# Attention and quantised feed-forward on one core: zero products in TensorE's idle times, quantisation moved into the setup, bias as a weight row, and later rows of maxima issued by SyncE

## What is computed

```python
x: [1, 2048, 128];  xn = layernorm(x)
# attention: 16 heads of dimension 8, causal the other way round (key >= query)
q, k, v = split(xn @ w_attn + b_attn)
scores = q @ k.T / sqrt(8) + mask        # mask = -log(1 + key - query), -inf where key < query
att = softmax(scores) @ v @ w_proj + b_proj
# feed-forward, all operands quantised to FP4 in blocks of 16 along the last dimension
quant(t): scale = max(max|block| / 6, 1e-12); grid value nearest |t| / scale, times sign and scale
gate = quant(xn) @ quant(w_gate).T       # w_gate, w_up: [352, 128]
up = quant(xn) @ quant(w_up).T
ffn = quant(silu(gate) * up) @ quant(w_down).T     # w_down: [128, 352]
out = x + att + ffn
```

## Time and profile before

| | us |
|---|---|
| median of 3 runs | 683.89 (682.28 to 686.52) |
| profiled execution | 685.19, of it 683.4 in the span of the trace |
| busy: PE, DVE, POOL, ACT | 587.4, 581.5, 509.0, 402.3 |
| mean granted clock of TensorE | 0.953 of 2.4 GHz |

### The profile page before, as it was taken

How to read it: one execution, slowest core, us unless ns; L and a number is a source line. 1 busy time by engine, 2 the same in 40 slices (tenths; PEclk the granted TensorE clock), 3 DMA queues, 4 the chain that set the end, 5 groups by cost and what they waited for, 6 DMA issues and landing times.

```text
span 683.4 us, 11295 instructions
## 1 busy us (share of the span) xinstructions
PE 587.4 (86%) x3788; PEld 264.4 (39%) x3839; DVE 581.5 (85%) x1206; ACT 402.3 (59%) x857; POOL 509.0 (74%) x386
## 2 busy tenths in 40 slices
PE   6998588668989798989898898989898898987895
PEld 6676354233434342433332342343234343342323
DVE  4786497999899999889999999999997999896462
ACT  3657146254565556566575666658564666667692
POOL 6034337885878887776879898789896798898893
PEclk9999799797999999999999999999998999999997
DMA  4344312201000000110000000000000000000000
GB/s 135 88 135 120 109 31 57 60 4 68 1 2 3 1 0 3 39 47 2 1 1 1 3 17 0 2 2 1 2 1 1 17 1 1 2 2 1 1 2 16
DMA packets 14717, 16.69 MB, mean 24 GB/s; under 512 B 1594, under 2 KB 14171, under 8 KB 14243
## 3 DMA queue, kind: packets, MB, share of 16 engines
q1 hardware_dynamic: 13859, 15.56, 8.2%
q10 hardware_dynamic: 800, 0.40, 0.2%
HBM read 11.75 MB, written 4.01 MB: 23 GB/s over the span
## 4 chain that ended last, share of the span: by engine, by line
PE 43%; POOL 23%; DVE 13%; ACT 8%; issue 7%; DMA 3%; ACTq 2%; SPq 1%; POOLq 0%; DVEq 0%
POOL ring L763 16%; PE psum L1357 10%; PE psum L1315 9%; PE psum L1339 7%; DVE mxp L1098 5%; DMA qop<-parts_dram 3%; ACT ring L915 3%; PE psum L1290 2%; PE psum L1207 2%; POOL xw L781 2%; POOL xw L779 2%; DVE ring L1125 2%; ACTq L927 2%; PE psum L1275 2%; POOL xw L783 2%
## 5 line engine op out<-in xcount | busy, mean ns | idle before, releaser
L763 POOL TENSOR_TENSOR ring<-ring,dist 128x1024 f32<-128x1024 f32 (+3 forms) x209 | 410.6, 1985 | 109.5 <-ACT ring L915 108.7
L1098 DVE TENSOR_REDUCE mxp<-psum 128x1 f32<-128x512 f32 (+3 forms) x640 | 356.3, 599 | 38.3 <-PE psum L1318 18.8
L915 ACT ACTIVATE ring<-psum 128x512 f32<-128x512 f32 (+3 forms) x418 | 199.7, 527 | 133.6 <-PE psum L1342 74.4
L1315 PE MATMUL psum<-kop,qop 96*128 96x512 bf16 (+3 forms) x640 | 205.3, 361 | 19.6 <-DMA qop<-parts_dram 7.4
L1339 PE MATMUL psum<-qop,kop 128*128 128x512 bf16 (+3 forms) x590 | 182.4, 354 | 20.6 <-ACT ring L915 7.9
L1357 PE MATMUL psum<-ring,vaug 128*32 128x512 f32 (+3 forms) x1280 | 154.1, 552 | 17.9 <-POOL ring L763 16.1
L915 ACT ACTIVATE psum<-psum 128x512 f32<-128x512 f32 (+3 forms) x222 | 113.2, 546 | 59.1 <-PE psum L1339 27.6
L1125 DVE TENSOR_TENSOR ring<-psum,dist 128x512 f32<-128x512 f32 (+3 forms) x222 | 133.5, 625 | 15.2 <-ACT psum L915 14.3
L1315 PEld LDWEIGHTS psum<-kop,qop 96*128 96x128 bf16 x640 | 58.3, 99 | 139.5 <-DVE mxp L1098 48.7
L1339 PEld LDWEIGHTS psum<-qop,kop 128*128 128x128 bf16 x640 | 59.9, 99 | 103.9 <-DVE ring L1125 24.0
L1318 PE MATMUL psum<-tri_q,identb 128*128 128x128 bf16 x256 | 57.3, 225 | 0.0
(11 more groups left out here) (132 smaller groups left out, 508.9 us busy)
## 6 DMA issues: line engine op xcount, KB each, us to landing
kop<-parts_dram SPq DMA_DIRECT2D x9, 384.0 KB
qop<-parts_dram SPq DMA_DIRECT2D x9, 384.0 KB
parts_dram<-qpart SPq DMA_DIRECT2D x18, 128.0 KB, 2.9
xin<-_attn_hidden_states_dram SPq DMA_DIRECT2D x4, 256.0 KB, 4.6
ring<-inv_dram SPq DMA_DIRECT2D x1, 1024.0 KB, 5.0
out_dram<-xin SPq DMA_DIRECT2D x4, 256.0 KB, 2.3
qop<-mrow ACTq DMA_DIRECT2D x48, 4.0 KB
parts_dram<-qpart SPq DMA_DIRECT2D x6, 96.0 KB
```

Of the source, the lines that this page charges most:

```text
L763: g_.tensor_tensor(slot(p)[:, :, 0:n], slot(p)[:, :, 0:n], both, ALU.mult).then_inc(weighed_pool, 1)
L915: a_.activation(scores if pair_vec[p] else slot(p)[:, e % 2, 0:n], scores, ACT.Exp, scale=SCALE).then_inc(exp_done, 1)
L1098: v_.tensor_reduce(mxp[:, u % 2, 4 * a + j, c - g:c - g + 1], bank(*o)[:, 0:n], AX_X, ALU.max).then_inc(max_used, 1)
L1315: ins = mm(bank(*o)[:, 0:n], qop[0:K_MAX, u // NQ % 2, h, P * a:P * (a + 1)], kop[0:K_MAX, h, k0:k0 + n], start=True, stop=(c != g))
```

## The change

1. PE may take products of zeros (`keep`, at most 4,000): a 128 by 128 bf16 tile of zeros with the identity, added to `OUT_BANK`. They have the last rank, and the plan takes one only where by its clock PE has had nothing for 200 ns and a unit's sum is open, that is between the first and the last `pv` of a unit. They wait for nothing.
2. Quantisation: no due time, rank 6.5 (a maximum has 4 when DVE is behind its schedule, 7 when it is ahead, a weighing 5); x pieces wait for their own transpose, the weights for their load; the order is x, x, weights, weights, x, x; the constant goes to the buffer of `hT` instead of `qc`, one buffer for all pieces; POOL's three operations are three items.
3. The bias of the last projection is loaded as row 97 of the third part of `wdT`, against a row of ones in `hT`; the product with `brow` goes.
4. From unit 5 on the rows of maxima are written by SP; SP's stream after the setup is ordered by the plan's times.
5. The plan's costs: `POOL_QUEUE` 3800 instead of 2600, and 1500 once all maxima are planned; 310 ns more for each `pv`, other costs for `minor`, `rows` and transfers.

```diff
-PIECES = [(S, WHALF), (S + WHALF, WHALF)] + [(S - GQ * (k + 1), GQ) for k in range(NG)]
+W_PIECES = [2, 3]
+X_PIECES = [0, 1, 4, 5]
+PIECES = {n: (S + WHALF * k, WHALF) for k, n in enumerate(W_PIECES)}
+PIECES.update({n: (S - GQ * (k + 1), GQ) for k, n in enumerate(X_PIECES)})
...
-FP4_AT, FP4_GAP = 80, 10
+FP4_RANK = 6.5
...
-POOL_QUEUE = 2600
+POOL_QUEUE, LAST_QUEUE = 3800, 1500
...
+KEEP, KEEP_AFTER = 4000, 200
...
+PV_SWITCH = 310
+ROWS_COPY, ROWS_ISSUE = 560, 620
...
-DMA_ROWS, DMA_HEADS, DMA_CHUNK = 6000, 8000, 17000
+DMA_ROWS, DMA_LATE_ROWS, DMA_HEADS, DMA_CHUNK = 6000, 4500, 8000, 17000
+ROWS_BY_ACT, OUT_SLACK = 5, 3000
...
-            needs = [("DVE", ("fp4", n, k - 1))] if k else [("POOL", ("fp4", n - 2))] if n >= 2 else []
-            needs += [("POOL", ("split", 2 * NG - 1, 1))] if n == 0 else [("PE", ("xnT", n - 2))] if n >= 2 else []
-            vec(("fp4", n, k), (GQ, 64, 64, GQ, GQ, GQ)[k], needs, at=FP4_AT + FP4_GAP * n, rank=3)
-        pool(("fp4", n), 3900, [("DVE", ("fp4", n, FP4_STAGES - 1))], rank=1)
+            needs = [("DVE", ("fp4", n, k - 1))] if k else [
+                ("PE", ("xnT", X_PIECES.index(n))) if n in X_PIECES else ("DMA", ("weights",))]
+            needs += [("POOL", ("fp4", n - 1, 1))] if k == 4 and n else []
+            vec(("fp4", n, k), (GQ, 64, 150, GQ, GQ, GQ)[k], needs, rank=FP4_RANK)
+        for k in range(3):
+            pool(("fp4", n, k), (1345, 1345, 1015)[k],
+                 [("POOL", ("fp4", n, k - 1)) if k else ("DVE", ("fp4", n, FP4_STAGES - 1))], rank=1)
...
-        pe(("xqT", k), 8 * P, [("POOL", ("fp4", 2 + k)), ("PE", ("v", NG - 1)), ("PE", ("qk", NG - 1, 1))], rank=3)
+        pe(("xqT", k), 8 * P, [("POOL", ("fp4", X_PIECES[k], 2)), ("PE", ("v", k)), ("PE", ("qk", k, 1))], rank=3)
...
+    for k in range(KEEP):
+        pe(("keep", k), P, [("PE", ("pv", 0))], rank=9)
...
-        pool(("minor", u), 900, [("DVE", ("parts", u, 1))], rank=0)
-        pe(("rows", u), 4 * P, [("POOL", ("minor", u))], rank=0)
-        act(("rows", u), GQ / 2, [("PE", ("rows", u))] + ([("DMA", ("rows", u - MROWS))] if u >= MROWS else []), n=5, rank=0)
+        pool(("minor", u), 740, [("DVE", ("parts", u, 1))], rank=0)
+        pe(("rows", u), 6 * P, [("POOL", ("minor", u))], rank=0)
+        add("ACT", ("rows", u), ROWS_COPY + (PARTS * ROWS_ISSUE if u < ROWS_BY_ACT else 0), 0,
+            [("PE", ("rows", u))] + ([("DMA", ("rows", u - MROWS))] if u >= MROWS else []), rank=0)
...
-        pe(("pv", s), 4 * P * blocks[s], needs, rank=5)
+        pe(("pv", s), 4 * P * blocks[s] + PV_SWITCH, needs, rank=5)
...
-        pe(("down", i), 16 * P, [("ACT", ("hT", i))], rank=1)
+        pe(("down", i), 12 * P, [("ACT", ("hT", i))], rank=1)
...
+    seen[("DMA", ("weights",))] = 52000
...
+            if kind == "keep":
+                return level if issued["open"] and now - issued["worked"] >= KEEP_AFTER else None
...
+        if engine == "PE" and kind != "keep":
+            issued["worked"] = now + took
+        if kind == "pv":
+            issued["open"] = item[1] != last_step[steps[item[1]][0]]
...
                 behind = max(clock["POOL"], now) + waiting["POOL"] - now
-                pair_vec[p] = behind > POOL_QUEUE
+                pair_vec[p] = behind > (LAST_QUEUE if work["max"] == total else POOL_QUEUE)
...
-            seen[("DMA", item)] = end + DMA_ROWS
+            seen[("DMA", item)] = end + (DMA_ROWS if item[1] < ROWS_BY_ACT else DMA_LATE_ROWS)
+            if item[1] >= ROWS_BY_ACT:
+                late.append((end, item))
...
+                late.append((end, ("q", u // NQ + 2)))
+        if kind in ("add", "sum"):
+            left_out[item[1] if kind == "add" else item[1] // TPG] -= 1
+            if left_out[item[1] if kind == "add" else item[1] // TPG] == 0:
+                late.append((end + OUT_SLACK, ("out", item[1] if kind == "add" else item[1] // TPG)))
...
-        busy = [e for e in queues if any(left[e].get(k, 0) < len(q) for k, q in queues[e].items())]
+        busy = [e for e in queues if any(k != "keep" and left[e].get(k, 0) < len(q) for k, q in queues[e].items())]
...
+    orders["SP"] = [o for _, o in sorted(late)]
...
+        qx = hT[:].rearrange("p a m n -> p (a m n)")
...
+        zerob = sb("zerob", [P, P], BF16)
...
-        qc = [sb(f"qc{i}", [P, WHALF], F32) for i in range(2)]
+        qc = [sb(f"qc{i}", [P, GQ], F32) for i in range(2)]
...
+        def load_rows(queue, u):
+            hq = parts_of(u)[1]
+            for i in range(PARTS):
+                queue.dma_start(qop[MROW + i:MROW + i + 1, u // NQ % 2, 4 * hq:4 * hq + 4, :],
+                                mrow[4 * i:4 * i + 4, u % MROWS, :]).then_inc(mrow_loaded[u % MROWS], 16)
...
-                    sp.dma_start(brow[:], b_proj.rearrange("(a n) -> a n", a=1)).then_inc(late_loaded, 16)
+                    sp.dma_start(wdT[F - 2 * P:F - 2 * P + 1, 2], b_proj.rearrange("(a n) -> a n", a=1)).then_inc(late_loaded, 16)
...
-            for gi, g in enumerate(GROUPS):
-                if gi + 2 < NG:
-                    last = (NQ * gi + NQ - 1, TPG * g)
+            for o in orders["SP"]:
+                if o[0] == "q":
+                    gi = o[1]
+                    last = (NQ * (gi - 2) + NQ - 1, TPG * GROUPS[gi - 2])
                     sp.wait_ge(st_psum, 4 * step_no[last] + 4)
-                    load_q(sp, gi + 2, 0, NH, qop_loaded[GROUPS[gi + 2]])
-                sp.wait_ge(fin_ready, gi + 1)
-                sp.wait_ge(down_used, TPG * (gi + 1))
-                sp.dma_start(out_t[:, TPG * g:TPG * (g + 1), :],
-                             xin[:, TPG * g:TPG * (g + 1), :]).then_inc(stored, 16)
+                    load_q(sp, gi, 0, NH, qop_loaded[GROUPS[gi]])
+                if o[0] == "rows":
+                    sp.wait_ge(mT_ready, o[1] + 1)
+                    load_rows(sp, o[1])
+                if o[0] == "out":
+                    gi, g = o[1], GROUPS[o[1]]
+                    sp.wait_ge(fin_ready, gi + 1)
+                    sp.wait_ge(down_used, TPG * (gi + 1))
+                    sp.dma_start(out_t[:, TPG * g:TPG * (g + 1), :],
+                                 xin[:, TPG * g:TPG * (g + 1), :]).then_inc(stored, 16)
             sp.wait_ge(stored, 16 * NG)
...
+            g_.memset(zerob[:], 0.0).then_inc(consts_ready, 1)
...
-                    n = o[1]
+                    _, n, k = o
                     x0, w = PIECES[n]
-                    v, c = xw[:, x0:x0 + w], qc[n % 2][:, 0:w]
-                    pool.wait_ge(round_ready, n + 1)
-                    g_.tensor_tensor(v, v, c, ALU.add).then_inc(fp4_seq, 1)
-                    pool.wait_ge(fp4_seq, 2 * n + 1)
-                    g_.tensor_tensor(v, v, c, ALU.subtract).then_inc(fp4_seq, 1)
-                    pool.wait_ge(fp4_seq, 2 * n + 2)
-                    blocks = v.rearrange("p (a b) -> p a b", b=BLK)
-                    g_.tensor_tensor(blocks, blocks, sc[:, x0 // BLK:(x0 + w) // BLK].rearrange(
-                        "p (a o) -> p a o", o=1).to_broadcast([P, w // BLK, BLK]), ALU.mult).then_inc(xwq_ready, 1)
+                    v, c = xw[:, x0:x0 + w], qx[:, 0:w]
+                    if k == 0:
+                        pool.wait_ge(round_ready, n + 1)
+                        g_.tensor_tensor(v, v, c, ALU.add).then_inc(fp4_seq, 1)
+                    if k == 1:
+                        pool.wait_ge(fp4_seq, 2 * n + 1)
+                        g_.tensor_tensor(v, v, c, ALU.subtract).then_inc(fp4_seq, 1)
+                    if k == 2:
+                        pool.wait_ge(fp4_seq, 2 * n + 2)
+                        blocks = v.rearrange("p (a b) -> p a b", b=BLK)
+                        g_.tensor_tensor(blocks, blocks, sc[:, x0 // BLK:(x0 + w) // BLK].rearrange(
+                            "p (a o) -> p a o", o=1).to_broadcast([P, w // BLK, BLK]), ALU.mult).then_inc(xwq_ready, 1)
+                        if n == len(PIECES) - 1:
+                            pool.wait_ge(xwq_ready, n + 1)
+                            g_.memset(hT[F - 2 * P:F - 2 * P + 1, :, 2], 1.0).then_inc(hones_ready, 1)
+                            pool.wait_ge(hones_ready, 1)
...
-                    hq = parts_of(u)[1]
-                    act.wait_ge(mT_ready, u + 1)
-                    for i in range(PARTS):
-                        act.dma_start(qop[MROW + i:MROW + i + 1, u // NQ % 2, 4 * hq:4 * hq + 4, :],
-                                      mrow[4 * i:4 * i + 4, u % MROWS, :]).then_inc(mrow_loaded[u % MROWS], 16)
+                    if u < ROWS_BY_ACT:
+                        act.wait_ge(mT_ready, u + 1)
+                        load_rows(act, u)
...
-                v, c, of = xw[:, x0:x0 + w], qc[n % 2][:, 0:w], slice(x0 // BLK, (x0 + w) // BLK)
+                v, c, of = xw[:, x0:x0 + w], qx[:, 0:w], slice(x0 // BLK, (x0 + w) // BLK)
...
-                    if n == 0:
+                    if n in W_PIECES:
                         vec.wait_ge(w_loaded, 16 * N_W)
```

(33 more changed lines are left out.)

12 lines of the change are left out of this document (5 added, 7 removed).

## The result

| | before | after |
|---|---|---|
| median of the runs, us | 683.31 (682.28 to 686.52, 4 runs) | 629.78 (629.02 to 629.94, 4 runs) |
| ratio | | 0.9207 [0.9175, 0.9239] |
| span of the profiled execution, us | 683.4 | 627.8 |
| mean granted clock | 0.953 | 0.983 |

The account below looks back on a forecast made before the run. The prediction took DVE as nearest to a bound from 119.5 to 615 us, with PE close behind. Its terms, -15 - 4 - 2 - 3 - 3 - 2 = -29 us, gave a median of 655 us, range 634 to 686.

Parts of the forecast that it names:

- Quantisation: Six pieces of DVE work move into idle time of the setup: -15 us, between -27 and -4.
- three quarters come through: Of 20 us taken off DVE after 119.5 us, three quarters shorten the kernel: -15 us.
- The contention part: Scaled product and mask run shorter in the setup, where POOL is less busy: 6.0 us of DVE's 27.3.
- Sharing and tail: POOL's longer queue takes 9 to 10 pairs from DVE, -4 us; a shorter limit near the end, -2 us.
- Rows by SP: Row transfers of 11 of 16 units leave ACT's queue: -3 us, between -9 and +5.
- ACT is busy about 60%, so most is slack: Of the 21 us of ACT's time freed from issuing row transfers, most would not shorten the kernel; -3 us taken.
- The clock and zero products: Zero products in PE's idle time: -5 us for the clock, +3 for delayed work, -2 us in sum.
- Bias: The last projection's bias as a weight row saves 6.6 us of PE: -3 us, between -6.6 and 0.
- Zero products in the way: Rival: zero products on PE's queue delay real work; with 1,800 of them +18, 702 us; chance 0.10.
- PE becomes the bound: Rival: from 119.5 us on PE's waits stay and only half the quantisation's gain arrives: -12, 672 us; chance 0.13.
- Rows late on SP: Rival: stores on SP's queue hold row loads back and PE waits for them: -5, 679 us; chance 0.08.
- Pieces do not move: Rival: rank 6.5 keeps the quantisation out of the setup until the loop: -8, 676 us; chance 0.07.

Follow-up runs that it names:

- late_fp4: The new kernel with the quantisation back at rank 3 and its old due times: 657.28 us, ratio 0.9616.
- old_limit: The new kernel with the limit of POOL's queue at 2600 throughout, 208 pairs on POOL instead of 222: 645.84 us, ratio 0.9435.
- fp4_limit_rows: The kernel before with the quantisation moved, the new limits of POOL's queue and rows by SP: 631.71 us, ratio 0.9222.
- zeros_at_once: The new kernel with zero products taken at once when the plan has PE idle, 849 instead of 123: 624.59 us, ratio 0.913.
- no_zeros: The new kernel planned without zero products: 626.55 us, ratio 0.9165.

## Why the prediction was right in direction and wrong in size

It was right that the kernel gets faster, and which parts would do it: quantisation, limits and rows are clear of an order's luck and have the sign that was forecast, each larger than forecast. Bias, zero products and costs are not clear of it. The sum was -29, measured -53.5. Undone one at a time, the parts of the new kernel are worth 27.5 + 16 + 8 to 12 + 1.7 + 0.5, which is 54 to 58. Two of the signs that it named failed: DVE is busy 95% from 119.5 to 560 us, not under 92%, since the loop became shorter with it, and POOL weighs 222 pairs, not 215 to 220.

**Quantisation, -15 forecast, 27.5 measured.** The places were read well: DVE's idle time in the setup fell by 19.1 us (14 forecast), and by the end of the fourth unit 16 maxima fewer were done than before, some 10 us displaced (7 forecast). The step that failed is "three quarters come through". late_fp4 shows the whole of 18.8 us arriving and 9.3 more: the time changes by more than the 20 us taken off DVE, where 15 were forecast. The reason for the discount was PE and POOL close behind a DVE that is 93% busy. But in the same 51 us PE was itself starved by the quantisation (37.96 of 51.30 us busy, clock 0.80), so its recovery came on top. I had named that and left it under this term without adding anything. That the recovery is all of the 9.3 is not shown. Whether the discount holds for the old kernel is open: there three runs give 12 to 13 us and the fourth 24. If it does hold, what the edit frees is kept only where the loop behind it can run faster.

The contention part (6.0 us shorter operations) was mis-sized: 27.3 fell to 25.3. The mask gave back 2.6 us (6.1 to 3.5; 3.6 forecast) and the scaled product 0.7 (7.8 to 7.1; 2.4 forecast), while the scale operation took 1.4 more (3.2 to 4.6): one of its six, of 32 columns, lasts 2.35 us from 73.37 on, beside a weighing of POOL from 73.34 to 75.68. POOL is now busy 62.91 us of the setup instead of 37.46. The new kernel's timeline shows the slowest of the six scaled products beside a weighing of POOL:

```profile
60.75 2.35 POOL L814 TENSOR_TENSOR ring<-ring,dist 128x1024 f32<-128x1024 f32 x1
61.34 2.36 DVE L1061 SCALAR_TENSOR_TENSOR xw<-xw,amax 128x560 f32<-128x560 f32 x1
```

The only other long one, 1.90 us at 77.44, has one beside it too (76.96 to 78.78); the other four take 0.68 to 0.78 us. Both long ones end some 0.6 us behind the weighing. That agrees with the rule of the Trainium skill that the prediction cites (SBUF — State Buffer, section Who interferes with whom): both inputs of the scaled product are in SBUF. The setup had room only until the change filled it. late_fp4, with the scaled products at a median of 1586 ns in the loop against 748, has the same DVE total, so the shorter operations bought nothing that can be seen.

**Sharing and tail, -4 and -2 forecast, 16 measured.** POOL took 13 pairs more instead of 9 or 10, and 26 heads at 0.624 are 16.2 us of DVE. The step that failed is the 9 us subtracted from a relief of 13 for later waits of PE for POOL. They did not come: PE's products with v wait 12.8 us for POOL in all of the new kernel, 16.1 before, and 20.0 in old_limit. That relief and gain are the same 16 is partly chance: with the old limit DVE is busy only 11.4 us longer, and its idle time makes up the other 5. On the old kernel alone it was 11.4. The tail's own limit of 1500 was never run by itself, so the two terms can't be told apart.

**Rows by SP, -3 forecast, 8 to 12 measured in the new kernel, 13 to 25 on the old one.** This is the worst step, "ACT is busy about 60%, so most is slack". The chain's 2% for ACT's queue was taken as the whole price. The earlier trace rows had the stall in view (1.99 us in which ACT computes nothing); I did not follow it to PE, whose banks are only freed by ACT. One stall with a fall of the clock is 1.9 us of ACT, 1.7 us of PE idle and then some 4 us near half clock, in which it does 2 us less: 3.7 us of PE. In the same orders 3 of 11 issues stall PE so, 2 of them with a fall; that is 8.6 us against 8 measured, and there the cause is shown, in kind and nearly in size. Of the 23 to 25 on top of quantisation and limits it explains the smaller part: 4 of 9 stands are ACT's, and the rest are PE's waits for POOL's quantisation and one for its weighing. The plan's cost for these items changed too (1.3 us before, against 0.57 + 1.83 in the trace), so its orders did not know of ACT's delay; the old kernel with that cost alone corrected was not run, and would tell.

**The clock and zero products, -2 forecast.** Not measurable: 1.3 us gained in the same orders, 3.2 lost against a plan without them, and on the old kernel 1.4 gained by the medians but 1.2 lost by the ratios, all within an order's luck. The clock of the loop rose to 1.00 without them: 0.985 with not a single zero product in fp4_limit_rows, where PE never stands for 1.3 us, and still 0.972 with 136 of them where it does. "Some hundreds" were 123.

**Bias, -3 forecast, 1.7 measured; plan's costs, 0 forecast, 0.5 measured.** Neither is clear of its interval (for the costs on the old kernel, 0.9532 against 0.9553).

**The rivals.** Zero products in the way: fell, 849 make the fastest kernel of all. PE becomes the bound: not in the form that I gave it; PE is busy 91%, but its share of the chain fell. From 170.8 to 560 us three engines are now within 8.4 us of each other: DVE 369.69 of 389.20 us, POOL 364.15, PE 361.33. POOL's share of the chain rose most, with pieces such as this one (start, us, what):

```profile
449.01 18.59 POOL ring L814 x8
```

Rows late on SP: fell, no wait of PE for them appears and the time improves in every pairing. Pieces do not move: fell (15 to 97 us).

**What the range missed.** The lower end of 634 joined the quantisation's bound of -27, which is about what was measured, with -10 for sharing (16 measured, with the tail) and -12 for all the rest. The terms were treated as shares of one chain that would each be damped by the next engine. They were not damped: alone on the old kernel they give 12.7 to 24, 11.4 and 13 to 15, together 53 to 55. Whether they help each other or only add depends on the 12.7 or 24, and stays open.

**A better version than the new kernel:** zeros_at_once (624.59) and no_zeros (626.55) are both below 629.78; since another order of the new kernel alone reaches 625.86 to 630.66, I would keep the simpler one and not claim the difference.

## What to carry to other kernels

Write the span as busy plus idle time of the engine that is nearest to full; here the work taken off it at 93 to 97% came through and its idle time fell besides, where stalls upstream went. An engine busy 60% has no slack if it can be blocked for 2 us while another engine works in order behind it: follow one such stall to its last victim, and the clock after it, before you price it from its share of the chain. Then list all the long stands of that engine before and after: only that shows how many were of the kind you followed. Try a part both added to the old and taken from the new kernel, and one neutral reordering, before a few microseconds are called an effect.
